# Products of a tile of zeros in TensorE's holes in the first microseconds of a macaron layer

## The reference

```
x = x + 0.5 * moe(layernorm(x))
x = x + attention(layernorm(x), WQ, WK, WV, WO)     # 16 heads of 8, causal
x = x + 0.5 * moe(layernorm(x))

def moe(x):                                    # 4096 tokens of 128
    probs = softmax(flat @ gate_w.T)           # 8 experts
    weights, idx = top_k(probs, 2)             # shares of the two, their sum is 1
    h1, h3 = flat @ w1[e].T, flat @ w3[e].T    # 256 hidden
    y = (silu(h1) * h3) @ w2[e].T
    return sum over the two experts of share * y
```

## Time and profile before

| | before |
|---|---|
| median of 3 executions | 622.59 us |
| the profiled execution | 619.24 us, span of its instructions 617.5 us |
| PE busy | 517.3 us (84%), 7286 matmul records |
| DVE busy | 374.3 us (61%) |
| ACT busy | 310.2 us (50%) |
| POOL busy | 267.6 us (43%) |
| mean granted TensorE clock | 0.973 |
| chain that ended last | PE 37%, DVE 16%, issue 4%, ACT 3% |

### The profile page before, as it was taken

The page is one execution under the profiler, slowest core; times in us unless marked ns, Lnnn a source line. Parts: engine busy times, 40 slices in busy tenths (PEclk is TensorE's granted clock), DMA queues, the critical chain, the costliest instruction groups (busy, mean ns, idle before and its releaser), DMA issues.

```text
span 617.5 us, 19023 instructions
## 1 busy us (share of the span) xinstructions
PE 517.3 (84%) x7286; PEld 416.7 (67%) x7286; DVE 374.3 (61%) x995; ACT 310.2 (50%) x597; POOL 267.6 (43%) x325
## 2 busy tenths in 40 slices
PE   1779879999998578888888886777689899999995
PEld 1667858779987345555556564545368789989994
DVE  5633933333355778888989988666346343355665
ACT  4853524344334156666666765556553244345543
POOL 6865764630654033434342110554614530556562
PEclk9999988999998679999999999999989999999999
DMA  9941223546865222656212020311033546653232
GB/s 275 329 150 39 53 68 91 137 108 145 154 151 144 72 60 72 170 155 189 90 50 85 16 88 2 115 36 37 31 74 93 144 124 122 152 131 99 66 90 56
DMA packets 114662, 65.87 MB, mean 107 GB/s; under 512 B 51856, under 2 KB 108432, under 8 KB 114576
## 3 DMA queue, kind: packets, MB, share of 16 engines
q1 hardware_dynamic: 107664, 50.49, 31.1%
q0 software_dynamic: 6912, 14.17, 8.6%
HBM read 18.88 MB, written 34.87 MB: 87 GB/s over the span
## 4 chain that ended last, share of the span: by engine, by line
PE 37%; DVE 16%; issue 4%; ACT 3%; another core or an unknown queue 1%; DMA 1%; POOL 0%; DVEq 0%; ACTq 0%; POOLq 0%
PE bank L1621 9%; DVE negmax L1302 7%; PE bank L1502 5%; PE bank L1504 5%; PE bank L1503 5%; PE bank L1734 2%; PE bank L1797 2%; ACT pt L950 2%; PE bank L1764 2%; PE bank L1812 1%; PE bank L1751 1%; PE bank L1800 1%; DVE rden L1319 1%; PE bank L1514 1%
## 5 line engine op out<-in xcount | busy, mean ns | idle before, releaser
L1189 DVE SCALAR_TENSOR_TENSOR pt<-bank,pt 128x512 f32<-128x512 f32 x122 | 84.3, 691 | 154.5 <-PE bank L1504 72.6
L694 POOL DMA_INDIRECT yg<-sorted_y,row x108 | 104.3, 965 | 145.8 <-PE bank L1621 65.7
L950 ACT ACTIVATE pt<-bank 128x768 f32<-128x768 f32 x128 | 103.8, 811 | 88.0 <-PE bank L1773 83.1
L680 POOL DMA_INDIRECT sorted_x<-xs,row x108 | 106.2, 983 | 78.9 <-DVE pt L1189 33.0
L1621 PE MATMUL bank<-w,pt 128*128 (+1 forms) x976 | 133.1, 279 | 8.5 <-issue 7.3
L1621 PEld LDWEIGHTS bank<-w,pt 128*128 128x128 f32 x976 | 120.5, 193 | 14.1 <-issue 10.0
L1302 DVE TENSOR_REDUCE negmax<-bank 128x10 f32<-128x640 f32 x128 | 104.2, 818 | 30.2 <-PE bank L1751 26.4
L833 ACT ACTIVATE pt<-bank 128x512 f32<-128x512 f32 x122 | 73.2, 600 | 50.0 <-PE bank L1504 37.3
L841 ACT ACTIVATE yb<-bank 128x256 f32<-128x256 f32 x82 | 31.5, 384 | 76.6 <-PE bank L1621 50.7
L1734 PE MATMUL bank<-zc 63*64 63x64 f16 (+3 forms) x1024 | 44.1, 250 | 30.4 <-DVE negmax L1302 24.8
L1734 PEld LDWEIGHTS bank<-zc 63*64 63x64 f16 x1024 | 19.3, 107 | 58.1 <-DVE negmax L1302 38.7
(11 more groups left out here) (171 smaller groups left out, 1022.6 us busy)
## 6 DMA issues: line engine op xcount, KB each, us to landing
sorted_y<-yb SPq DMA_DIRECT2D x82, 128.0 KB
zc<-qk_rows SPq DMA_DIRECT2D x96, 64.0 KB
sorted_x<-zeros SPq DMA_DIRECT2D x2, 2944.0 KB, 14.1
qk_rows<-qksplit SPq DMA_DIRECT2D x8, 512.0 KB
sorted_x<-zeros SPq DMA_DIRECT2D x1, 2432.0 KB, 11.5
sorted_x<-zeros SPq DMA_DIRECT2D x1, 2176.0 KB, 10.2
X<-x_in SPq DMA_DIRECT2D x8, 256.0 KB, 5.1
zc<-w_up SPq DMA_DIRECT2D x8, 256.0 KB, 6.1
```

Of the source, the lines that this page charges most:

```text
L680: ps.indirect_dma_start(out=sorted_x[s], out_offset=bass.IndirectOffsetOnAxis(ap=row[:, s, k, t:t + 1], axis=0), in_=xs[:, R0[s] + t, :], ...
L694: ps.indirect_dma_start(out=yg[:, a % D_YG, k, :], out_offset=None, in_=sorted_y[s], in_offset=bass.IndirectOffsetOnAxis(ap=row[:, s, k, t ...
L950: s_.activation(pt[:, hg, (u % 2) * 768:(u % 2 + 1) * 768].rearrange("p (a n) -> p a n", a=2), bank[:, B_ST:B_ST + 2, 0:384], ACT.Exp, sca ...
L1189: v_.scalar_tensor_tensor(hid[:, n % D_HID], bank[:, B_H3 + n % 2, :], 1.0 / WSCALE, silu[:, n % D_H], ALU.mult, ALU.mult).then_inc(prod_d ...
```

## The change

PE gets a helper `keep_warm(n, b0)`: n products of the first 128 columns of `zeros` (stationary) with all its 256 columns (moving), into the first 256 columns of bank `b0`. Nobody reads them, they carry no semaphore, and bank 4 (`B_Y[0]`) is in no other use before the first `down`. There are 64 of them ahead of T(0), after a wait for the memset of `zeros` alone, 6 ahead of each T(g) from g = 1 on (42 in all), 32 between G(3) and `sums(0)`, and 10 after `block_parts(0, 0)`: 148.

```diff
+            def keep_warm(n, b0):
+
+                for _ in range(n):
+                    t_.matmul(bank[:, b0, 0:2 * D], zeros[:, 0:D], zeros[:, :], start=True, stop=True)
+
...
+            pe.wait_ge(consts, 1)
+            keep_warm(64, B_Y[0])
             pe.wait_ge(consts, 6)
             pe.wait_ge(w_lo, 1)
             transpose_first(0)
             for g in range(1, GROUPS):
                 if g == 5:
+                    keep_warm(32, B_Y[0])
                     pe.wait_ge(consts, 15)
                     sums(0)
+                keep_warm(6, B_Y[0])
                 transpose_first(g)
                 gate_first(g - 1)
                 if g >= 6:
                     block_parts(0, g - 6)
+                if g == 6:
+                    keep_warm(10, B_Y[0])
             pe.wait_ge(rg_copied, GROUPS - 1)
             dense_up(0, 0)
```

## The result

The changed kernel took 626.07 us (median of 20 executions, 622.13 to 631.9), the kernel before 623.34 us (20 executions beside them, 621.27 to 626.25). The ratio is 1.004 with a 95% interval of 1.0021 to 1.0058: a small loss, within 1%, where a gain of 6.9 us was forecast. It is outside the stated range of 611.5 to 623.5.

What follows compares the result with a forecast made beforehand. The prediction took the head to be bound by a chain of handovers with PE at the low clock. Its steps summed to 6.9 us earlier at the first `down`, 622.59 - 6.9 = 615.7 us, range 611.5 to 623.5.

Steps and rivals of the forecast that it cites:

- The first 64 products: Ahead of T(0): 21 slow and 43 fast, 9.2 us ending at 10.3, covered by the wait for ACT.
- The rival that products of zeros never raise the clock: Whole head stays at the low clock with the added products: 12.3 us lost, 634.9 us; chance 0.11.
- Six a turn keep the clock up and are covered: Before T(1) to T(4): 0.65 us of products each time, fitting a 2.68 us turn at the high clock.
- the second rival: Clock falls again between T(1) and G(3): only 1.6 us gained, 621.0 us; chance 0.14.
- Step 1: G(3) takes 1.06 instead of 1.88 us at the high clock, so logits, `chosen` and `sums(0)` come 0.82 us earlier.
- Steps 2 to 4: From `sums(0)` to G(7) at the high clock: lead grows from 0.82 to 4.1 us at G(7)'s start, 4.8 after it.
- Step 5: Between G(7)'s end and DVE's read of the last logits: unexplained 2.3 us wait kept unchanged; logits 4.8 us earlier.
- The worst case that the prediction set for it: A stretch of 5.7 us in place of the 2.3 us wait for the last logits, leaving 3.5 us gained.
- Step 6: `dense_up(0, 1)` and `(0, 2)` take 2.62 instead of 4.77 us, so the first `down` starts 6.9 us earlier.
- What the head gains should shift everything behind it: Behind the first `down`: the head's 6.9 us arrive at the end, unless POOL's scatters fall behind.
- The first rival: Scatters in a longer row slow PE in units 1 to 3: 3.5 us gained, 619.1 us; chance 0.14.
- The sign: Total time against the kernel before: faster 0.44, same 0.42, slower 0.14.

Runs made afterwards that it cites:

- e3: Changed kernel with 8 columns instead of 256 in each of the 148 products: 623.65 us, ratio 0.9986 to the kernel before.
- e2: Changed kernel without the 24 indirect DMAs of set 0 (part of the computation left out): 618.0 us, ratio 0.9877 to the kernel before.
- e1: Kernel before without the 24 indirect DMAs of set 0 (part of the computation left out): 612.76 against 623.55 us, ratio 0.985.
- e10: Kernel before with only POOL's scatters of set 0 from number 8 on waiting for DVE's multiplies: 617.48 against 618.18 us, ratio 0.9986.
- e7: Changed kernel with 10 products ahead of T(1) to T(4), none ahead of T(5) and T(6), 20 more behind G(7): 624.66 us, ratio 1.0011 to before.
- e6: Changed kernel with 20 more products between G(7) and the wait for the last logits: 629.22 us, ratio 1.0131 to the kernel before.
- e12: Kernel before with the 24 indirect DMAs of set 0 replaced by plain DMAs of 64 KB from POOL's queue: 611.58 against 617.68 us, ratio 0.9893.
- e13: Kernel before with each of the 24 indirect DMAs of set 0 replaced by a POOL memset of about 0.9 us: 612.5 us, ratio 0.9898.
- e8: The kernel of e7 without the 24 indirect DMAs of set 0 (part of the computation left out): 610.08 us, ratio 0.9801 to the kernel before.
- e9: The kernel of e7 with POOL's scatters of set 0 from number 8 on waiting for DVE's multiplies: 620.59 us, ratio 1.0043 to the kernel before.
- e5: Changed kernel with 10 products instead of 6 ahead of T(1) to T(4): 625.28 us, ratio 1.0045 to the kernel before.
- e4: Changed kernel with only the 64 products ahead of T(0), all others taken out: 623.83 us, ratio 0.9969 to the kernel before.

## Why the prediction was wrong, by its own steps

**The first 64 products: right.** They were put at 9.2 us, ending at 10.3; they took 8.53 us and ended at 9.68, hidden under the wait for ACT. The rival that products of zeros never raise the clock is out. With 8 columns in place of 256 (e3) the clock rose only where it did before.

**Six a turn keep the clock up and are covered: wrong.** This is the first step that failed; its opposite was the second rival, with 0.14. The clock fell at 17.65. Step 1's gain of 0.82 us at G(3) became a loss of some 0.5 us (its end at about 25.1 against 24.6), and the 32 products, taken as 3.5 us with 1 us to spare, took 5.05 us and put `sums(0)` 0.93 us later than before; in e2 they took 6.37 us and put it 3.8 us later than in e1. The rival had said 4.5 us late for the latter: too much for this profile, nearly right for e2. The Trainium skill (page "TensorE: Matmul & The Clock Gate", part 4, PE-mode transpose) had transposes not counting as a busy PE; the trace agrees in so far as 4.79 us of PE work in 6.60 us, with T's and G's among it, did not hold the high level.

**Steps 2 to 4: right in size.** From `sums(0)` to `block_parts(0, 0)` it took 4.20 us after against 5.55 before; forecast were 4.5 (5.55 - 0.32 - 2.03 + 1.31). T took 0.60 to 0.66 us, G 0.96 to 1.06, the 12 products of `dense_up(0, 0)` 1.32 us (forecast 1.31). G(7) starts 2.7 us earlier; the forecast was 4.1, and what had already failed ahead of these steps was 0.82 + 0.93 = 1.75 of it, which leaves 2.4. The size was met with every one of these products at the high level.

**Step 5, a hold of 2.3 us kept as it was: right there by luck, wrong as a treatment.** Between G(7)'s end (41.5) and DVE's read (43.85) there are 2.4 us after. That is luck, since it ended in another way: before, POOL's row had ended at 45.79 when the logits were read at 47.17; after, the row went on. In e10 and e7 the same read isn't held at all. So the price was no property of G(7), and it had to be asked what happens to it when POOL stops pausing. The worst case that the prediction set for it, 5.7 us, isn't worked out there; its own row of the first routed tile gives 7.2 - 1.3 = 5.9 us.

**Step 6, 24 products in 2.62 us: wrong.** They took 4.30 us (44.10 to 48.40), because the clock fell at 45.0, behind the hole in which PE waited for the held logits. The hold isn't the only way to such a fall: in e2, without any, the clock was low from 41.8, and in e6 from 41.1. The forecast had the clock high once raised. Steps 1 to 6 together: 3.8 us instead of 6.9.

**"What the head gains should shift everything behind it": the step that failed most.** The first rival named the mechanism, scatters in a longer row holding PE's results back, and priced it at 3.4 us with 0.14. Between the first `down` and the 14th multiply 3.8 + 3.0 = 6.8 us were lost. Of these 5.2 are gone by the tenth multiply (72.32 against 70.91), the stretch with the holds; the other 1.6 come with units 10 to 13, where nothing is held and the clock was low from 72.3 to 75.7. That the indirect DMAs are the cause of the holds is shown by e1, e12 and e13 on the kernel before and by e7 against e8 with a short head: of 7.8 us of lead at the first `down` 0.6 are left at the 14th multiply in e7, while e8 keeps its 2.4 us over e1 in full. That a pause of POOL lets the others through is supported by e10, where an earlier pause did away with the hold behind G(7), and by e7, before and e9, where ACT or DVE goes on 1.4 us after the row's end; the two holds of the changed kernel that ended inside its row show that the pause isn't needed for it. The prediction had this pause in the earlier trace rows and read it as slack; an earlier multiply of unit 0 took it away. Against this rival it set a row of four or five that shows nothing like it, and it passed over a third place that does: unit 4 of its own trace (silu at 59.33), beside a row of eight.

**The sign.** Without scatters the change still loses in the head, 3.3 us at the 14th multiply (e2 against e1), so slow fillers alone were enough for a loss there. With them, the two can't be separated by subtraction, because the holds swallow what the head gains (e5 and e7 keep the clock up for longer and end at 1.0045 and 1.0011). What is shown: with longer fillers and no holds (e8) the idea is worth 2.4 us at the 14th multiply, and whether that reaches the end is open; with the holds no form of it gained time. Why the changed kernel is 2.7 us slower, and not level with the kernel before, is followed only to the 14th multiply, where its trace is 3.0 us late.

**What stays open.** In e9 and e10 the 14th multiply is 4.6 and 3.6 us early and the medians are +2.4 and -0.7 us. In e9's trace the lead is lost in the attention part: from the first `negmax_t` to the last it takes 231.2 us, in e7 232.2, and 223.4 to 227.4 in the other fourteen traces. PE's clock may be part of it. Busy time by stretch, e9 and then before:

```profile
190.00:215.00 25.00, 17.55 (x311) 11.78 (x310) 18.20 (x37) 7.87 (x14) 4.33 (x6) 0.69 0.32 92
...
330.00:455.00 125.00, 99.03 (x2199) 65.97 (x2198) 86.95 (x242) 74.75 (x117) 41.87 (x51) 0.96 0.16 48
```

```profile
190.00:215.00 25.00, 18.61 (x250) 14.07 (x248) 18.37 (x34) 8.08 (x16) 4.24 (x5) 0.77 0.35 98
...
330.00:455.00 125.00, 98.03 (x2236) 65.43 (x2232) 88.48 (x242) 76.06 (x117) 41.74 (x51) 0.99 0.16 49
```

The granted clock is 0.69 against 0.77 and 0.96 against 0.99. The two traces weren't taken side by side, and e10, nearly as early at the 14th multiply, is not among the long ones (226.1 us); why e7 and e9 meet a lower clock there is not settled, as no run changed the attention part.

## What to carry to other kernels

Filling an engine's holes to keep its clock up needs fillers for every hole on the way, the last one too, and each filler has to be costed at the low clock as well, since the fillers are what stands in the way when the clock has fallen. Before a gain in one stretch is passed on to the end, ask what the other engines' pauses in that stretch were good for: here POOL paused because PE was slow, and without that pause the waits for PE grew to 4 and 7 us. A wait whose two ends the trace can't connect is to be taken as a mechanism with its own trigger, not as a constant of the place where it was seen.

## What the runs showed of the hardware

- While POOL works through a row of indirect DMAs, engines that wait for PE go on up to some 8 us late (e7: ACT at 50.60 for products finished by 42.2, the semaphore's event recorded at 50.57), often 1.4 us after the row's end (before, e7, e9), but in the changed kernel twice while the row went on. PE's own products come late too (e7: eight in 3.8 us, e8: in 1.06). Leaving out 24 indirect DMAs of 0.96 us gave 10.8 us of 623.55 by the medians and 9.4 by the ratio (e1); with 24 plain DMAs of the same 64 KB or 24 memsets of 0.95 us in their place the kernel was 6.1 and 5.2 us faster. The intervals of the three ratios overlap. Why this is so no run shows.
- Products of a zero tile raise the clock like others: it rose at 4.0 us, with nothing but them on PE since 1.15. With 148 products of 8 columns (e3) it rose at 51.96, and before at 51.8.
- Between executions of the changed kernel the time goes with the mean granted clock: over the 20 of them a clock lower by 0.01 goes with 3.4 us more (correlation -0.8), without the two longest with 2.8 us (-0.7). That doesn't say which of the two brings the other. From one kernel to another it tells little: e4's profiled execution had the lowest mean clock of all, 0.938, and e4 was as fast as before. The record begins only with the first change of the clock, so the slow head of before isn't counted as slow.
